# Eight of thirteen field pairs spread by DMA instead of seven, with a new order of the dump, the row loads, the gathers and the first tile

## The chip, the cores and the metric

The kernel runs on one core of one Trainium2 chip. The metric is the time of one execution on the device in microseconds (us), as the median of several runs. The engines of a core are TensorE (PE), VectorE (DVE), ScalarE (ACT), GpSimd (POOL) and SyncE (SP, which only issues DMAs here). Sixteen DMA engines move data between the chip's memory (HBM) and the core's SBUF. TensorE writes its results to PSUM.

## The reference, cut to what matters

It is an xDeepFM recommender with a batch of 2048, 26 sparse fields with embeddings of 32 numbers, and 13 dense numbers:

```python
emb = tables[feat_idx, sparse]                      # (2048, 26, 32)
linear_out = lin_sparse_w[feat_idx, sparse].sum(-1) + dense @ lin_dense_w
x0 = emb; xk = emb; res = []
for w, bb in ((conv1_w, conv1_b), (conv2_w, conv2_b)):
    h = xk.shape[1]                                 # 26, then 64
    hp = einsum('bhd,bmd->bhmd', xk, x0).reshape(-1, h * M, E)
    xn = sigmoid(einsum('oi,bid->bod', w, hp) + bb[None, :, None])
    half = xn.shape[1] // 2                         # 64
    xk = xn[:, :half]
    res.append(xn[:, half:])
cin_out = (concatenate(res, axis=1).sum(-1) @ cin_w + cin_b)[:, 0]
h1 = tanh(deep_x @ W1 + b1)                         # 845 -> 1024, deep_x is emb and dense
h2 = tanh(h1 @ W2 + b2); h3 = tanh(h2 @ W3 + b3)    # 512, 256
return linear_out + cin_out + (h3 @ deep_w + deep_b)[:, 0] + bias[0]
```

The second layer's products dominate: for each batch row and each of 32 embedding places, 64 values of `xk` times 26 of `x0`, contracted with a 128 x 1664 matrix. All is float32.

## The kernel before

**Tiles and steps.** The batch is cut into 16 tiles of 128 rows, and each tile into 4 steps of 8 embedding places (`STEP_D`); a step has 8 x 128 = 1024 columns. In a step, both halves of the 128 partitions hold the 64 values of `xk`, and one of 13 *pairs* of fields is laid beside them: the first field of the pair for one half of the partitions, the second for the other. So a pair takes one DVE multiplication of 128 x 1024 (L747) and a contraction on PE (`contract`, L800), which adds all 13 pairs into one accumulator. `ORDER` says which fields a pair number stands for.

**Laying out a pair.** The fields' values have to be repeated over 64 partitions. For the pairs in `BY_PE` PE does that with a matmul by 0/1 weights from the rows `x0t` into a PSUM slot `bc` (`spread_pair`, L780), from a 32-row quarter for each half of the columns (`group_of` says which quarters). DVE reads the slot and writes `hp`. For the pairs in `BY_DMA` the SP queue copies the field's row of 4 KB from HBM (`x0_rows`) into each of 64 partitions of `xb` (`spread_by_dma`, L501), in four groups (`COPIED`); DVE multiplies in place. The buffer of a pair is free when it has been contracted, and only then SP asks for the next step's copy (`sp.wait_ge(contracted, ...)`).

**The K part.** The first layer is symmetric, so it is computed from squares of sums of two fields: `spread_sum` (L787) fills three slots (`("K", 0..2)`), ACT squares them (L979), and PE contracts them in two column halves (`contract_k`, L794, "first"). ACT reads each half with a sigmoid (`read_xn`, L984 to L986): twice into `xk` for the next step and once into `r1`. PE's contractions of the step's own first five pairs ("of_this") wait for the read of half 0 (`xn_read`), since they start the accumulator that it frees. `read_y2` (L990) reads the finished accumulator of the step before into `r2`; the second K half waits for it. POOL adds up `r1` and `r2` (`add_up`).

**The order on PE** is written out in `STEP_WORK`: K fills, contractions 5 to 7 of the step before, turning the next tile's embeddings ("D"), contractions 8 to 12, pairs 0 to 2 spread, K contraction in two halves, pairs 5 to 7 spread, contractions 0 to 4. The slots `bc` are used in turn (`SLOTS` is 3).

**The next tile.** POOL gathers 26 fields of 128 rows into `emb` (L572), each gather tied to a multiplication (`gather_in`). In one step of a tile (`deep_step`: step 2 of the first tile, step 1 of the others; none in the last) PE transposes `emb` (`turn_deep`, L772) in three fills. ACT copies the result to `deep_t` and, rounded to float32r, to `deep_halves` (L975, L976), DVE computes the remainder (`lower_deep`, L698). SP then writes `deep_t` to `x0_rows` (`dump`, L438) and ACT writes both halves to `x0_halves` (`dump_halves`, L997, L999), ahead of its read of K half 1 in steps 1. From `x0_halves` ACT's queue loads `x0t` two steps ahead (`load_rows`, L388), four DMAs a step. In step 2 of a tile these are the first rows of the next tile, and they wait for the dump (`halves_dumped`); ACT issues them there behind `read_y2`.

**Queues.** Each engine works its instructions in order, the issue of DMAs too. SP: per step the four groups of spreads, then the row dump, and in the last two tiles the loads of `x_full` and `x_rest` (`load_x`, L490) for the deep layers, which run after all tiles.

## Time and profile before

| | |
|---|---|
| median of 3 runs | 1602.87 us (1598.68 to 1613.62) |
| the profiled execution's own time | 1607.53 us |
| its span | 1605.7 us |
| PE / DVE / ACT / POOL busy | 94% / 71% / 40% / 43% of the span |
| DMA moved | 322.08 MB, mean 201 GB/s |

The profile is one execution. "Busy" of an engine is the time in which it works an instruction; idle time is given with the instruction before which it stood, and with what ended it. The DMA share is the mean busy share of the 16 DMA engines. A step of a tile is measured from one K fill (L787) to the next; the first K fill of step 1 of tile 0 is at 80.30 us, and step 0 of tile 1 opens at 148.89.

### The profile page before, as it was taken

Reading aid. Unit: us, or ns where it says so; the run is one execution under the profiler, and the core shown is the slowest. Engines: PE = TensorE matmul, PEld = TensorE weight load, DVE = VectorE, ACT = ScalarE, POOL = GpSimd, SP = SyncE. Lnnn points to the kernel's source line nnn. Section 1 sums busy time; section 2 is a strip of 40 time slices with the busy share of each in tenths; the row PEclk is TensorE's granted clock in tenths of the full one; section 3 lists DMA queues with packets and bytes.
Section 4 is the critical chain, followed back from the end, with each engine's and each line's share of the span. In section 5 each row is a group of like instructions: output and inputs, shape, how many; then the busy total and the mean of one; then the engine's idle time right before and its main releaser. Section 6 shows DMA issues by size and latency. Waiting matters only on the chain.

```text
span 1605.7 us, 23632 instructions
## 1 busy us (share of the span) xinstructions
PE 1515.2 (94%) x6552; PEld 662.5 (41%) x6552; DVE 1133.7 (71%) x1113; ACT 646.7 (40%) x904; POOL 682.6 (43%) x600
## 2 busy tenths in 40 slices
PE   0598999999999999999999999999999999999999
PEld 0233333333333333333333333333333337787876
DVE  3385878788888887878787877788876785343442
ACT  2333443444444344334444443434443433444443
POOL 7356564546464646454555546464631010000000
PEclk9998999999999999999999999999999999999999
DMA  6686989888998899988898989898999993846741
GB/s 130 132 228 170 230 217 222 197 232 204 241 216 233 201 232 198 233 200 232 206 241 208 236 198 236 203 247 200 246 194 240 234 243 105 187 129 167 166 134 53
DMA packets 177869, 322.08 MB, mean 201 GB/s; under 512 B 30160, under 2 KB 106032, under 8 KB 177796
## 3 DMA queue, kind: packets, MB, share of 16 engines
q1 hardware_dynamic: 128250, 287.98, 70.8%
q10 hardware_dynamic: 36273, 26.61, 6.9%
q0 software_dynamic: 13312, 7.06, 4.4%
q8 instruction: 18, 0.29, 0.1%
q14 instruction: 16, 0.13, 0.0%
HBM read 300.24 MB, written 21.31 MB: 200 GB/s over the span
## 4 chain that ended last, share of the span: by engine, by line
PE 75%; DMA 9%; issue 4%; DVE 3%; SPq 2%; ACTq 2%; POOL 2%; ACT 1%; another core or an unknown queue 0%; DVEq 0%; POOLq 0%
PE acc L800 37%; PE acc L794 16%; PE bc L937 14%; DMA x0t<-x_halves 6%; PE bc L780 4%; PE bc L787 3%; ACTq L388 2%; POOL emb L572 2%; DMA emb<-table,idx_stage 2%; SPq L490 1%; DVE xb L747 1%; DVE hp L747 1%; DMA x_halves<-deep_halves 1%; PE bc L772 1%; DMA xb<-x_rows 1%
## 5 line engine op out<-in xcount | busy, mean ns | idle before, releaser
L572 POOL DMA_INDIRECT emb<-table,idx_stage x416 | 494.8, 1189 | 335.9 <-DVE hp L747 169.9
L747 DVE TENSOR_TENSOR hp<-bc,xk 128x1024 f32<-128x1024 f32 x384 | 446.3, 1217 | 257.1 <-PE bc L780 172.7
L747 DVE TENSOR_TENSOR xb<-xb,xk 128x1024 f32<-128x1024 f32 x448 | 552.4, 1288 | 15.1 <-DMA xb<-x_rows 14.9
L800 PE MATMUL acc<-xb,w2s 128*64 128x512 f32 x1792 | 408.6, 594 | 0.2
L800 PE MATMUL acc<-hp,w2s 128*64 128x512 f32 x1536 | 362.9, 608 | 6.0 <-ACT r L986 6.0
L794 PE MATMUL acc<-sq,w1s 128*128 128x512 f32 x768 | 349.9, 605 | 2.2 <-issue 2.2
L979 ACT ACTIVATE sq<-bc 128x1024 f32<-128x1024 f32 x192 | 182.9, 1027 | 190.2 <-PE bc L787 144.0
L800 PEld LDWEIGHTS acc<-xb,w2s 128*64 128x64 f32 x1792 | 127.1, 137 | 253.3 <-issue 227.0
L583 POOL TENSOR_TENSOR r<-r 128x512 f32<-128x512 f32 x96 | 128.8, 1342 | 220.6 <-ACT r L990 130.3
L794 PEld LDWEIGHTS acc<-sq,w1s 128*128 128x128 f32 x768 | 141.9, 191 | 181.3 <-issue 181.3
L984 ACT ACTIVATE xk<-acc,bias 64x512 f32<-64x512 f32 x128 | 87.3, 682 | 275.9 <-PE acc L794 164.1
L800 PEld LDWEIGHTS acc<-hp,w2s 128*64 128x64 f32 x1536 | 99.9, 138 | 202.8 <-issue 164.2
L990 ACT ACTIVATE r<-acc,bias 128x512 f32<-128x512 f32 x64 | 44.0, 687 | 285.5 <-PE acc L800 266.9
L937 PE MATMUL bc<-x_full,w_hi 128*128 128x512 f32 x384 | 125.2, 394 | 5.0 <-DVE w_lo L712 2.0
L762 DVE TENSOR_TENSOR h_lo<-h_raw,h_hi 128x512 fp32r<-128x512 f32 x48 | 33.2, 692 | 135.7 <-ACT h_hi L1109 135.7
L780 PE MATMUL bc<-x0t,sel 32*128 32x512 f32 x768 | 94.3, 462 | 5.4 <-ACT sq L979 4.2
L986 ACT ACTIVATE r<-acc,bias 64x512 f32<-64x512 f32 x128 | 87.4, 683 | 3.2
L1107 ACT ACTIVATE h_raw<-bc,bd 128x512 f32<-128x512 f32 x48 | 33.1, 689 | 137.1 <-PE bc L937 137.1
L985 ACT ACTIVATE xk<-acc,bias 64x512 f32<-64x512 f32 x128 | 87.1, 681 | 1.6
L787 PE MATMUL bc<-x0t,sel 64*128 64x512 f32 x384 | 63.0, 433 | 25.8 <-DMA x0t<-x_halves 14.2
L937 PEld LDWEIGHTS bc<-x_full,w_hi 128*128 128x128 f32 x384 | 72.2, 188 | 23.5 <-issue 7.1
L780 PEld LDWEIGHTS bc<-x0t,sel 32*128 32x128 f32 x768 | 38.1, 183 | 105.6 <-issue 57.9
(61 smaller groups left out, 814.0 us busy)
## 6 DMA issues: line engine op xcount, KB each, us to landing
xb<-x_rows SPq DMA_DIRECT2D x448, 256.0 KB
xb<-x_rows SPq DMA_DIRECT2D x192, 512.0 KB
w_raw<-W SPq DMA_DIRECT2D x48, 512.0 KB
xb<-x_rows SPq DMA_DIRECT2D x128, 128.0 KB
x0t<-x_halves ACTq DMA_DIRECT2D x252, 52.0 KB
x_full<-x_halves SPq DMA_DIRECT2D x96, 128.0 KB
x_halves<-deep_halves ACTq DMA_DIRECT2D x30, 384.0 KB
emb<-table,idx_stage POOLq DMA_INDIRECT x416
```

The lines of the kernel that those rows point to most:

```text
L572: nc.gpsimd.indirect_dma_start(out=emb[:, m, :], out_offset=None, in_=table, in_offset=bass.IndirectOffsetOnAxis(ap=idx_stage[:, m:m + 1], ...
L583: nc.gpsimd.tensor_tensor(total, r[:, 0, :] if sl == 1 else total, r[:, sl, :], ALU.add).then_inc(step, 1)
L747: nc.vector.tensor_tensor(product(n)[:, :], x[:, :], xk[sl % 2][:, :], ALU.mult).then_inc(multiplied, 1)
L780: last = nc.tensor.matmul(bc[slot][:, c * CHUNK:(c + 1) * CHUNK], sel[rows, ORDER[n], :], x[rows, :], start=True, stop=True)
L787: last = nc.tensor.matmul(bc[slot][:, c * CHUNK:(c + 1) * CHUNK], sel[rows, PAIRS + k, :], x[rows, :], start=True, stop=True)
L794: last = nc.tensor.matmul(acc_k[:, :], w1s[:, k, :], sq[k][:, cols], start=(k == 0), stop=(k == K1 - 1))
L800: last = nc.tensor.matmul(acc_y[H * c:H * c + H, :], w2s[:, ORDER[n], :], src[:, c * CHUNK:(c + 1) * CHUNK], start=(n == 0), stop=(n == PA ...
L937: last = nc.tensor.matmul(bc[a % 2][:, 0:CHUNK], w, x, start=(k == 0 and i == 0), stop=(k == rows - 1 and i == len(passes) - 1))
L979: nc.scalar.activation(sq[k][:, :], bc[slot][:, :], ACT.Square).then_inc(squared, 1)
L984: nc.scalar.activation(xk[slot][0:H, cols], xn[0:H, :], ACT.Sigmoid, bias=bias1[0:H, :])
L985: nc.scalar.activation(xk[slot][H:P, cols], xn[0:H, :], ACT.Sigmoid, bias=bias1[0:H, :]).then_inc(xk_made, 1)
L986: nc.scalar.activation(r1[H * c:H * c + H, sl, :], xn[H:P, :], ACT.Sigmoid, bias=bias1[H:P, :]).then_inc(xn_read, 1)
```

## The change

`BY_PE` becomes (0, 1, 2, 5, 6) and `BY_DMA` has eight pairs in four groups of two, (3, 4), (7, 8), (9, 10), (11, 12); `ORDER` is rearranged so that neighbouring PE pairs still lie in different quarters. The second spread of a step is one pair shorter. The turn of the embeddings is one fill of one slot instead of three (`TURNS`). It is in step 1 of every tile that has one, also of the first, which gets an order of its own there (`FIRST_TILE_WORK`), and DVE lowers the halves behind its multiplication 4 in that step. In the first tile the dump of the halves is issued by SP, behind the first spread of step 2; in the others by ACT, now directly behind `read_y2` and so ahead of both K reads. The row loads of step 2 stand ahead of `read_y2`. The gathers are timed anew and end a step earlier. One of the dense remainders moves from an `hp` buffer to `xb[7]`, and SP waits for its dump before the first tile.

```diff
@@ -63,10 +63,10 @@
 PER_GROUP = 16
-ORDER = [0, 8, 1, 3, 4, 9, 2, 10, 5, 6, 7, 11, 12]
-BY_PE = (0, 1, 2, 5, 6, 7)
+ORDER = [0, 8, 1, 3, 4, 9, 2, 5, 6, 7, 10, 11, 12]
+BY_PE = (0, 1, 2, 5, 6)
 assert sorted(ORDER) == list(range(PAIRS))
-COPIED = ((3, 4), (8, 9), (10, 11), (12,))
+COPIED = ((3, 4), (7, 8), (9, 10), (11, 12))
 BY_DMA = tuple(n for ns in COPIED for n in ns)
@@ -75,45 +75,59 @@
 STEP_WORK = (
     ("fill", (("K", 0), ("K", 1), ("K", 2))),
-    ("of_last", (5, 6, 7)),
-    ("fill", (("D", 0), ("D", 1), ("D", 2))),
-    ("of_last", (8, 9, 10, 11, 12)),
+    ("of_last", (5, 6, 7, 8)),
+    ("fill", (("D", 0),)),
+    ("of_last", (9, 10, 11, 12)),
     ("fill", (0, 1, 2)),
     ("first", 0),
     ("first", 1),
-    ("fill", (5, 6, 7)),
+    ("fill", (5, 6)),
     ("of_this", (0, 1, 2, 3, 4)),
 )
 FINAL_WORK = (
     ("fill", (0, 1, 2)),
     ("of_last", (5, 6, 7, 8, 9, 10, 11, 12)),
-    ("fill", (5, 6, 7)),
+    ("fill", (5, 6)),
     ("of_this", (0, 1)),
     ("terms", None),
     ("of_this", (2, 3, 4)),
 )
+
+FIRST_TILE_WORK = (
+    ("fill", (("K", 0), ("K", 1), ("K", 2))),
+    ("of_last", (5, 6, 7, 8)),
+    ("of_last", (9, 10, 11, 12)),
+    ("fill", (0, 1, 2)),
+    ("first", 0),
+    ("fill", (("D", 0),)),
+    ("first", 1),
+    ("of_this", (0, 1)),
+    ("fill", (5, 6)),
+    ("of_this", (2, 3, 4)),
+)
+DEEP_STEP = 1
 LEFT = tuple(n for kind, what in STEP_WORK if kind == "of_last" for n in what)
 DEEP_PARTS = range(0, 3), range(3, KD - 1), range(KD - 1, KD)
+
+TURNS = ((0, 1, 2),)
 SLOTS = 3
 PRO_FILLS = 6
 DUMPS = 2
 HALF_DUMPS = 3
-def deep_step(ahead):
-
-    return 2 if ahead == 3 else 1
+def step_work(sl, ahead):
+
+    if ahead == 0 and sl == STEPS - 1:
+        return FINAL_WORK
+    return FIRST_TILE_WORK if ahead == 3 and sl == DEEP_STEP else STEP_WORK
 def step_fills(sl, ahead):
-    fills = [use for kind, what in STEP_WORK if kind == "fill" for use in what]
-    if ahead == 0 and sl == STEPS - 1:
-        fills = [use for use in fills if not is_k(use)]
-    if ahead == 0 or sl != deep_step(ahead):
-        fills = [use for use in fills if not is_d(use)]
-    return fills
+    fills = [use for kind, what in step_work(sl, ahead) if kind == "fill" for use in what]
+    return fills if ahead > 0 and sl == DEEP_STEP else [use for use in fills if not is_d(use)]
 def is_k(use):
@@ -239,7 +253,7 @@
         diag_w = xb_all[0:M, 0:2 * M * P]
         diag = xb_all[0:M, 2 * M * P:(2 * M + 1) * P]
         dense_hi = [hp[2 + i][0:ND, :].bitcast(F32R) for i in range(2)]
-        dense_lo = [hp[4 + i][0:ND, :].bitcast(F32R) for i in range(2)]
+        dense_lo = [x[0:ND, :].bitcast(F32R) for x in (hp[4], xb[7])]
         x0t = [sc(f"x0t{i}", [P, CHUNK], F32R) for i in range(STEPS)]
@@ -388,6 +402,14 @@
                 eng.dma_start(x0t[sl][start:start + 2 * M:2, :].bitcast(F32),
                               rows[:, first:first + Q, :].rearrange("m d b -> m (d b)")).then_inc(x0_loaded[sl % 2], 16)
+
+        def dump_halves(eng, t):
+            for i in range(2):
+                eng.dma_start(x0_halves[bass.ds(t, 1), i, 0:(KD - 1) * P, :].rearrange("t (k p) b -> p (t k) b", p=P),
+                              deep_halves[:, i, 0:KD - 1, :].bitcast(F32)).then_inc(halves_dumped, 16)
+            eng.dma_start(x0_halves[bass.ds(t, 1), :, (KD - 1) * P:M * ROW, :].rearrange("t i p b -> p (t i) b"),
+                          deep_halves[0:LAST_E, :, KD - 1, :].bitcast(F32)).then_inc(halves_dumped, 16)
+
         W1_STEPS = 6
@@ -508,7 +530,11 @@
                             sp.wait_ge(contracted, contracted_by(s - 1, ns[-1]))
                             hold()
                         spread_by_dma(t, sl, i)
-                    if sl == deep_step(ahead) and ahead > 0:
+                        if is_first and sl == DEEP_STEP + 1 and i == 0:
+                            sp.wait_ge(deep_lowered, 2 * DEEP_N)
+                            hold()
+                            dump_halves(sp, t + 1)
+                    if sl == DEEP_STEP and ahead > 0:
                         dump(t + 1)
@@ -529,6 +555,7 @@
                 load_rows(sp, 0, sl, 0)
             sp.wait_ge(w1_step, W1_STEPS)
+            sp.wait_ge(dense_dumped, 64)
             sp.wait_ge(first_rows, FIRST_ROWS)
@@ -612,40 +639,42 @@
                 if is_first:
                     free_emb(t, DEEP_N)
                     gather(range(8), gathered)
-                    gather_in(s, range(8, 16), range(8))
+
+                    for m, (signal, count) in enumerate(((k_contracted, 1), (xk_made, 1), (xk_made, 2), (squared, K1 + 1),
+                                                         (squared, K1 + 2), (squared, 2 * K1))):
+                        pool.wait_ge(signal, count)
+                        hold()
+                        gather((8 + m,), gathered)
+                    gather_in(s, range(14, M), (0, 1, 2, 3, 4, 4, 4, 4, 5, 6, 7, 8))
                     add_up(t, 1, r1, r1_step, xn_read, 2, sum1)
-                    gather_in(s, range(16, 21), range(8, PAIRS))
-                    gather_in(s + 1, range(21, M), range(5))
                     add_up(t, 2, r1, r1_step, xn_read, 2, sum1)
+                    free_emb(t + 1, filled_by(t, DEEP_STEP, ("D", len(TURNS) - 1), ahead))
                     add_up(t, 1, r2, r2_step, y2_read, 1, sum2)
-                    free_emb(t + 1, filled_by(t, 2, ("D", DEEP_N - 1), ahead))
                     gather_in(s + 2, range(5), (1, 2, 3, 4, 6))
                     add_up(t, 3, r1, r1_step, xn_read, 2, sum1)
                     gather_in(s + 2, range(5, 11), range(7, PAIRS))
                     add_up(t, 2, r2, r2_step, y2_read, 1, sum2)
-                    gather_in(s + 3, range(11, 20), range(9))
+                    gather_in(s + 3, range(11, 22), (0, 1, 1, 2, 3, 3, 4, 5, 6, 7, 7))
                     return
                 if ahead > 0:
-                    gather_in(s - 1, range(20, 23), (8, 10, 12))
+                    gather_in(s - 1, range(22, M), (8, 9, 10, 12))
                 add_up(t - 1, STEPS - 1, r2, r2_step, y2_read, 1, sum2)
-                if ahead > 0:
-                    gather_in(s, range(23, M), (0, 1, 3))
                 add_up(t, 1, r1, r1_step, xn_read, 2, sum1)
                 if ahead > 1:
-                    free_emb(t + 1, filled_by(t, 1, ("D", DEEP_N - 1), ahead))
+                    free_emb(t + 1, filled_by(t, 1, ("D", len(TURNS) - 1), ahead))
                     gather_in(s + 1, range(4), (0, 2, 4, 6))
                 add_up(t, 2, r1, r1_step, xn_read, 2, sum1)
                 if ahead > 1:
                     gather_in(s + 1, range(4, 8), (7, 8, 10, 12))
                 add_up(t, 1, r2, r2_step, y2_read, 1, sum2)
                 if ahead > 1:
-                    gather_in(s + 2, range(8, 11), (0, 2, 4))
+                    gather_in(s + 2, range(8, 12), (0, 2, 4, 6))
                 add_up(t, 3, r1, r1_step, xn_read, 2, sum1)
                 if ahead > 1:
-                    gather_in(s + 2, range(11, 15), (7, 8, 10, 12))
+                    gather_in(s + 2, range(12, 17), (7, 8, 9, 10, 12))
                 add_up(t, 2, r2, r2_step, y2_read, 1, sum2)
                 if ahead > 1:
-                    gather_in(s + 3, range(15, 20), (0, 2, 4, 6, 7))
+                    gather_in(s + 3, range(17, 22), (0, 2, 4, 6, 7))
             over_tiles(pool, tile)
@@ -726,7 +755,7 @@
                     s = t * STEPS + sl
                     start = is_first and sl == 0
                     for n in range(PAIRS):
-                        if n == 0 and sl == deep_step(ahead) and ahead > 0:
+                        if n == (5 if is_first else 0) and sl == DEEP_STEP and ahead > 0:
                             dve.wait_ge(gathered, t * GATHERED + GATHERED)
...
@@ -828,7 +857,7 @@
                 else:
                     if use[1] == 0:
                         pe.wait_ge(gathered, t * GATHERED + GATHERED)
-                    turn_deep(slot, DEEP_PARTS[use[1]])
+                    turn_deep(slot, [k for part in TURNS[use[1]] for k in DEEP_PARTS[part]])
             pe.wait_ge(ident_loaded, IDENT_LOADED)
...
@@ -968,10 +997,11 @@
             upper_w(0, 0)
-            def turned_deep(slot, part):
+            def turned_deep(slot, part, first_k):
                 ks = DEEP_PARTS[part]
                 rows = rows_of(ks)
-                src = bc[slot][rows, 0:len(ks) * P].rearrange("p (k b) -> p k b", b=P)
+                at = (ks[0] - first_k) * P
+                src = bc[slot][rows, at:at + len(ks) * P].rearrange("p (k b) -> p k b", b=P)
                 nc.scalar.activation(deep_t[rows, ks[0]:ks[-1] + 1, :], src, ACT.Copy).then_inc(deep_copied, 1)
@@ -989,20 +1019,10 @@
                 act.wait_ge(contracted, s * PAIRS + PAIRS)
                 nc.scalar.activation(r2[:, sl, :], acc[sl % 2][:, :], ACT.Sigmoid, bias=bias2[:, :]).then_inc(y2_read, 1)
-
-            def dump_halves(t):
-                act.wait_ge(deep_lowered, t * DEEP_N + DEEP_N)
-                act.sem_inc(act_held, 1)
-                for i in range(2):
-                    act.dma_start(x0_halves[bass.ds(t, 1), i, 0:(KD - 1) * P, :].rearrange("t (k p) b -> p (t k) b", p=P),
-                                 deep_halves[:, i, 0:KD - 1, :].bitcast(F32)).then_inc(halves_dumped, 16)
-                act.dma_start(x0_halves[bass.ds(t, 1), :, (KD - 1) * P:M * ROW, :].rearrange("t i p b -> p (t i) b"),
-                             deep_halves[0:LAST_E, :, KD - 1, :].bitcast(F32)).then_inc(halves_dumped, 16)
-
             act.wait_ge(ident_loaded, IDENT_LOADED)
             for i in range(DEEP_N):
                 act.wait_ge(filled, i + 1)
-                turned_deep(i, i)
+                turned_deep(i, i, DEEP_PARTS[i][0])
             act.wait_ge(first_halves, FIRST_HALVES)
@@ -1020,10 +1040,6 @@
                     s = t * STEPS + sl
                     start = is_first and sl == 0
                     there = step_fills(sl, ahead)
-                    turning = sl == deep_step(ahead) and ahead > 0
-
-                    late = turning and sl == 2
-
                     def load_next_rows():
@@ -1033,8 +1049,8 @@
                             for c in range(2):
                                 load_rows(act, t + (sl + 2) // STEPS, (sl + 2) % STEPS, c)
-                    for kind, what in STEP_WORK:
-                        if kind == "of_last" and what[-1] == PAIRS - 1 and ("K", 0) in there and sl != 2:
+                    for kind, what in step_work(sl, ahead):
+                        if kind == "of_last" and what[-1] == PAIRS - 1 and ("K", 0) in there:
                             load_next_rows()
@@ -1051,23 +1067,19 @@
                                         else:
                                             act.wait_ge(dumped, t * (16 * DUMPS))
                                             act.wait_ge(halves_dumped, t * (16 * HALF_DUMPS))
-                                    turned_deep(slot_of(sl, use, ahead), use[1])
+                                    for part in TURNS[use[1]]:
+                                        turned_deep(slot_of(sl, use, ahead), part, DEEP_PARTS[TURNS[use[1]][0]][0])
                         elif kind == "of_last" and what[-1] == PAIRS - 1 and not start:
                             if sl == 1 and not is_first:
                                 act.wait_ge(r2_step, t * SUMS - (SUMS - 1))
                             if sl == STEPS - 1 and not is_first:
                                 act.wait_ge(r2_step, t * SUMS - (SUMS - (STEPS - 1)))
-                            if late:
-                                dump_halves(t + 1)
                             read_y2(s - 1, (sl - 1) % STEPS)
-
-                            if sl == 2 and not late:
-                                load_next_rows()
+                            if sl == DEEP_STEP and ahead > 0 and not is_first:
+                                act.wait_ge(deep_lowered, t * DEEP_N + 2 * DEEP_N)
+                                act.sem_inc(act_held, 1)
+                                dump_halves(act, t + 1)
                         elif kind == "first" and ("K", 0) in there:
-                            if turning and not late and what == 1:
-                                dump_halves(t + 1)
-                            if late and what == 1:
-                                load_next_rows()
                             act.wait_ge(k_contracted, k_contracted_by(s, what))
```

## Rows read from the trace of the kernel before

**Rows 1.** The page: busy shares, and groups with busy, mean ns, idle before.

```profile
PE 1515.2 (94%) x6552; PEld 662.5 (41%) x6552; DVE 1133.7 (71%) x1113; ACT 646.7 (40%) x904; POOL 682.6 (43%) x600
...
L747 DVE TENSOR_TENSOR xb<-xb,xk 128x1024 f32<-128x1024 f32 x448 | 552.4, 1288 | 15.1 <-DMA xb<-x_rows 14.9
...
L780 PE MATMUL bc<-x0t,sel 32*128 32x512 f32 x768 | 94.3, 462 | 5.4 <-ACT sq L979 4.2
```

**Rows 2.** The timeline of PE in one step: start us, us, what, idle before.

```profile
602.33 0.98 PE L787 MATMUL bc<-x0t,sel 64*128 64x512 f32 x6 [1.39 <-DMA x0t<-x_halves]
...
610.25 0.73 PE L780 MATMUL bc<-x0t,sel 32*128 32x512 f32 x6
610.91 5.42 PE L794 MATMUL acc<-sq,w1s 128*128 128x512 f32 x12
```

**Rows 3.** Windows by step: length, busy PE PEld DVE ACT POOL, PEclk, DMA share, GB/s.

```profile
99.33:126.95 27.62, 20.16 (x91) 7.49 (x90) 21.70 (x22) 9.33 (x16) 6.22 (x7) 0.93 0.84 235
126.95:148.89 21.94, 21.93 (x82) 7.74 (x82) 9.78 (x9) 7.89 (x11) 15.57 (x16) 0.86 0.57 137
...
542.00:561.03 19.03, 19.03 (x86) 6.84 (x84) 14.97 (x14) 7.63 (x10) 13.42 (x11) 1.00 0.93 201
561.03:581.25 20.22, 20.16 (x93) 7.47 (x91) 16.39 (x18) 9.09 (x16) 4.34 (x5) 1.00 0.85 195
581.25:602.33 21.08, 19.16 (x85) 6.83 (x83) 18.05 (x15) 8.15 (x11) 15.09 (x12) 1.00 1.02 260
602.33:621.36 19.03, 19.03 (x82) 6.83 (x82) 14.18 (x13) 7.63 (x10) 11.57 (x11) 1.00 0.88 212
```

**Rows 4.** Windows of twelve tiles and of the last two; queues: packets, MB, share.

```profile
208.29:1151.35 943.06, 929.12 (x4022) 335.61 (x4022) 757.57 (x672) 390.01 (x552) 519.14 (x444) 1.00 0.90 220
1151.35:1310.00 158.65, 155.85 (x669) 55.53 (x667) 121.66 (x109) 63.04 (x86) 39.49 (x36) 0.99 0.99 225
...
q1 hardware_dynamic: 62891, 181.47, 75.2%
q10 hardware_dynamic: 28644, 20.78, 9.1%
```

**Rows 5.** Waits of PE in the same twelve tiles: us in total, times, longest.

```profile
PE bc L787 <- DMA x0t<-x_halves: 6.8, 8, 1.7
PE acc L800 <- ACT r L986: 4.1, 3, 2.8
```

**Rows 6.** Windows of two steps beside the x loads, columns as in 3.

```profile
1210.23:1233.84 23.61, 21.50 (x86) 6.99 (x84) 15.08 (x15) 8.95 (x12) 5.00 (x5) 0.93 1.05 255
...
1271.89:1290.92 19.03, 19.03 (x85) 6.83 (x83) 14.91 (x15) 7.64 (x10) 1.27 (x1) 1.00 1.08 246
```

**Rows 7.** Timeline of ACT, its queue and PE in a step 1; line L999 (min/median/max ns).

```profile
570.25 0.69 ACT L990 ACTIVATE r<-acc,bias 128x512 f32<-128x512 f32 x1 [2.78 <-PE acc L800]
...
575.52 4.03 ACTq L999 DMA_DIRECT2D x_halves<-deep_halves  x1
...
576.80 2.80 PE L800 MATMUL acc<-hp,w2s 128*64 128x512 f32 x12
...
579.67 0.68 ACT L984 ACTIVATE xk<-acc,bias 64x512 f32<-64x512 f32 x1 [3.76 <-issue]
...
L999 ACTq DMA_DIRECT2D x_halves<-deep_halves x15: 1053/3597/6312, 107.4 to 1203.8; - x15
```

**Rows 8.** The chain that ended last, around 593 us: start, us, what.

```profile
593.31 8.97 DMA x0t<-x_halves
```

**Rows 9.** The first tile: a piece of the chain; the timeline of POOL and ACT.

```profile
107.38 14.39 DMA x_halves<-deep_halves
...
69.94 0.95 POOL L572 DMA_INDIRECT emb<-table,idx_stage  x1 [15.47 <-DVE hp L747]
71.19 0.95 POOL L572 DMA_INDIRECT emb<-table,idx_stage  x1 [0.30 <-issue]
...
125.13 0.68 ACT L984 ACTIVATE xk<-acc,bias 64x512 f32<-64x512 f32 x1 [11.20 <-issue]
```

4 lines of the change are left out of this document (2 added, 2 removed).

## The prediction

> **What bounds the kernel now.** I read the busy shares first: TensorE (PE) 94%, VectorE (DVE) 71%, ScalarE (ACT) 40% [rows 1]. The timeline of PE inside one step of the product part shows it going from the fill of the K part through contractions, a spread of three pairs (0.73 us), the K part's 12 matmuls and on, without idle time but the one before the fill [rows 2]. The table by step gives 19.03 us for steps 0 and 3 of a tile and 20.22 for step 1, which also turns the next tile's embeddings (1.2 us of it, seven transposes); with 19.03 for step 2 a tile would be 77.3 us [rows 3]. Twelve whole tiles took 943.06 us, 78.6 each, at a DMA share of 0.90 [rows 4]. So PE sets 77.3 of 78.6 us. The DMA engines are the second resource: 0.90 x 78.6 = 70.7 us of work of all 16 per tile. By step [rows 3] (share times length, scaled by 70.7/73.2 to the mean tile) it is 17.1, 16.6, 20.8 and 16.2 us; step 2, with the dump of the next tile, is at 1.02. The waits of PE in those tiles are mostly 6.8 us for loads of x0t and 4.1 us for ACT's reads [rows 5].
>
> **One pair less on PE.** Three pairs are spread in 0.66 us (610.25 to 610.91) by 6 matmuls [rows 2]. At 462 ns each [rows 1] one after another they would take 2.8 us, so those of different row quarters run together; neighbouring pairs lie in opposite halves, hence three pairs are two rounds of 0.33 us and two pairs one. I take 0.33 us a step (bounds 0.22, a third of 0.66, and 0.33). The pair's contraction stays. A tile's floor on PE becomes 77.3 - 1.3 = 76.0 us. DVE multiplies the pair from SBUF instead of PSUM, one instruction either way; it is busy 15.0 of 19.03 us [rows 3], and that idle time covers a small difference: nothing.
>
> **One pair more by DMA.** The SP queue, q1, takes 75.2% of 943.06 us, 14.8 us in each of 48 steps, and moves 181 MB [rows 4]. Twelve row dumps of 429 KB are 5 MB of them, so seven pairs are 14.4 us and one is 2.05 us of all engines. A tile's work becomes 70.7 + 8.2 = 78.9 us, against a floor of 76.0. What decides is how much work the engines do per microsecond of time. Shares of 1.05 and 1.08 were held for 19 to 24 us, beside x loads in small pieces, and 1.02 in a step 2 [rows 3, 6]. I take 1.03, nearest to that last row, which has the same mix (bounds 1.00 and 1.08).
> In bytes: those three stretches moved 246 to 260 GB/s, and eight pairs make 220 GB/s x 19.65 us + 0.52 MB = 4.85 MB a step, 18.7 to 19.7 us. The Trainium skill, page "DMA: Bandwidth & Descriptors", section "Specifications", gives about 358 GB/s as the HBM limit of one core; by it the same bytes would need an estimated 13.5 us and the change would go as in the first rival. No row here comes near that rate over a step, and the sum goes by the rows.
>
> **ACT's dump moved ahead of its first read.** Now ACT reads y2 (570.25) and xk's half 0, and then issues the three DMAs of the halves' dump. The third holds ACT's queue for 4.03 us, so that half 1 is read only at 579.67, 3.76 us late [rows 7]. Nobody waits for half 1 then. Over 15 tiles that issue takes 1.05 to 6.3 us, 3.6 in the median [rows 7]. In the new order all three stand between the read of y2 and that of half 0, and PE's contractions 0 to 4 wait for exactly this read (`xn_read`). From 570.9 (570.25 and its 0.69): 1.3 us for the first two issues, as they end before the third at 575.52, and 3.6 make 575.8; three activations of 0.7 end at 577.9. PE would be ready at 576.80 - 0.33 = 576.5 [rows 7]. That is 1.4, and I take 1.5 us a tile in step 1. Bounds: 0, if the issue holds the queue as little as its minimum of 1.05, and 4.5, if it ends no sooner than now. Behind it in ACT's queue stands the read of half 1, which nobody awaits, and the squares of the K fill at 581.25, which it doesn't reach but at the upper bound.
> What the move buys: the dump's data flow earlier. The ACT queue, q10, works 9.1% of the stretch, 7.2 us a tile, and half its bytes are the dump [rows 4]; up to 3.6 us of DMA work leaves step 2 for step 1, and I take half, 1.8. In step 2 the loads of the next tile's first x0t no longer stand behind the read of y2, about 9 us into the step, but behind three squares, about 5 us sooner. Now the last of them is issued at 593.31 and lands at 602.28 for a fill due at 600.9 [rows 2, 8]. That stall, 6.8 us in twelve tiles, goes; late next are the spreads of xb.
>
> **Middle tile, summed.** Step 0: DMA 19.2/1.03 = 18.6, so PE's 18.7, and 18.8 with some unevenness. Step 1: DMA (18.6 + 1.8)/1.03 = 19.8; PE 20.2 - 0.33 + 1.5 = 21.4. Step 2: (22.8 - 1.8)/1.03 = 20.4, of which 0.4 is caught up in step 3: 20.0. Step 3: DMA 17.7, so PE's 18.7. Together 78.9 against 78.6, +0.3: over 13 tiles **+4 us** (with the bounds of its terms it is the rivals' tile).
>
> **First tile.** Its turn moves from step 2 to step 1. Step 2 is 27.62 us now: the dump's last DMA takes 14.39 us to land, ACT stands 11.20 us for it. Step 3 is 21.94 us, with the granted clock at 0.86 after that idle time [rows 3, 9]. In the new order step 1 gains the turn (19.03 + 1.2 - 0.33 = 19.9). The dump goes out on SP after the first spread of step 2, at about 101.5 to 104, and lands 5 to 14 us later; ACT waits for it ahead of y2, so x0t is asked for at 110 to 118, and of that the 11 us until PE wants y2 cover the first part. I take 22.0 for step 2 and 18.7 for step 3: 27.62 + 21.94 + 19.03 = 68.6 become 60.6, **-8 us** (bounds -3, the dump as slow as now, and -11, no wait left). The gathers must now be done at about 91, not 103. POOL idles 15.47 us before the ninth; six are moved into that gap, and at 0.95 + 0.30 us each the other twelve end near 85 [rows 9]: nothing, unless they land over 5 us later, which would cost PE what is over. Behind the dump in SP's queue are pairs 7 and 8; they slip about 4 us and are due 13 us after they are free: nothing. SP's new wait for the dense dumps is for transfers of the start, long landed when it is reached: nothing.
>
> **Gathers and groups.** The last gathers of later tiles end a step sooner. The pairs (7, 8) are asked for after contraction 8 and needed after seven multiplications, no tighter than (8, 9) now. Nothing for both.
>
> **Last two tiles.** Here SP also loads x: 0.99 x 158.65 = 157.1 us of work [rows 4]. Eight steps with one pair more add 16.4; at 1.05, the share of these steps [rows 6], 165.2 us, **+6.5** (bounds -8, PE alone and the excess of the 23.61 us step gone, and +15, share 1.00).
>
> Sum: +4 - 8 + 6.5 = +2.5 on the profiled execution's 1607.5, 1610. The median of the runs shown is 4.7 us under that execution, hence **1605**. The deep layers that follow aren't touched.
>
> **Rivals**, all against the median.
> 1. Faster: the engines carry the eighth pair as they carry seven, and ACT's wait is nil. Middle tile 76.2 (-2.4 x 13), first -11, last two -8: -50, **1553**. For it: the ordinary steps' shares of 0.85 to 0.93, and the 1.08. Against: 1.02 in step 2 already. It is also the page's rule. 0.22.
> 2. Faster: as forecast, but ACT's queue isn't held. Step 1 is 19.9, a tile 77.4: -16 - 8 + 5, **1584**. Against it stands the median of 3.6 us. 0.12.
> 3. Slower: the engines give a share of 1.00. Its place is DVE's wait for xb. A tile is 19.2 + 21.4 + 21.0 + 18.7 = 80.3, +22; first -7; last two +15: +30, **1633**. It decides from a share under about 1.02. For it: 0.90 is all that the middle tiles show on average, and spreads can only be asked for when their buffer is free. 0.22.
> 4. Slower: ACT's third issue ends where it ends now, 3 us more in 14 tiles, +42: **1647**. 0.10.
> The forecast's own case has 0.34 and spans 1590 to 1619.
>
> What a measurement of this kernel can tell from no change is about 1%, 1587 and 1619. Faster: rivals 1 and 2 but for an edge, 0.32. Slower: rivals 3 and 4, 0.32. Same: 0.36. The range cuts rivals 1 and 4 by half each: 1554 to 1646.
>
> **What would show it.** Right: DVE's idle time for DMA xb, 14.9 us now [rows 1], grows beyond 50; the DMA share of the middle tiles is 1.00 or more; PE waits 1 to 2 us for ACT's r once a tile, in step 1; spreads of two pairs take 0.33 us; waits for x0t are gone behind the first tile; the K fill that opens tile 1 comes near 141 us, not at 148.89. Wrong: tiles of 76 us at a share below 1 are rival 1; a step 1 of 24 us is rival 4; a first tile that waits for gathers breaks its term.

## The result, and the profile after

The changed kernel takes 1699.26 us (median of 4 runs, 1682.09 to 1706.57), the kernel before 1604.05 us beside it: a ratio of 1.057, 95% interval 1.048 to 1.067. It is about 90 us slower, not the same. The profiled execution took 1699.54 us; its span is 1697.7 us against 1605.7. (In the experiments below some executions were disturbed ones, which no ratio uses, among them the profiled ones of two kernels, the one with the dump behind both K reads and the first with the row loads a step earlier; of these only the pattern of steps and issues is used.)

The page of the changed kernel; columns as in [rows 1] (L776 is DVE's multiplication, L829 the contraction, L809 the spread of pairs on PE):

```profile
PE 1539.3 (91%) x6424; PEld 661.7 (39%) x6424; DVE 1159.8 (68%) x1113; ACT 646.5 (38%) x904; POOL 678.2 (40%) x600
...
L776 DVE TENSOR_TENSOR xb<-xb,xk 128x1024 f32<-128x1024 f32 x512 | 651.1, 1327 | 48.7 <-DMA xb<-x_rows 43.0
...
L829 PE MATMUL acc<-hp,w2s 128*64 128x512 f32 x1280 | 331.0, 650 | 69.4 <-ACT r L1016 65.7
...
L809 PE MATMUL bc<-x0t,sel 32*128 32x512 f32 x640 | 80.6, 482 | 5.5 <-ACT sq L1009 4.2
```

DVE waits longer for the copies (43.0 us, from 14.9), as an eighth pair by DMA would let one expect. But the new item is the third line: PE stands 65.7 us in front of contractions of `hp`, the pairs 0 to 2, and what releases it is ACT's read of the K part's half 0. It was 4.1 us in twelve tiles [rows 5] and 6.0 us in the whole execution before.

The windows of the changed kernel, columns as in [rows 3]: steps 0 to 3 of a middle tile, the long step 1 near the end, the thirteen tiles 1 to 13, and step 2 of the first tile.

```profile
568.30:587.10 18.80, 18.80 (x82) 6.72 (x80) 15.38 (x14) 7.64 (x10) 11.13 (x10) 1.00 1.02 246
587.10:613.40 26.30, 21.66 (x89) 7.74 (x87) 22.88 (x22) 9.60 (x16) 7.90 (x8) 0.94 0.86 228
613.40:632.20 18.80, 18.80 (x82) 6.72 (x80) 10.00 (x9) 7.63 (x10) 7.90 (x8) 1.00 0.95 232
632.20:651.00 18.80, 18.80 (x82) 6.69 (x80) 17.05 (x14) 7.64 (x10) 15.52 (x14) 1.00 0.98 250
...
1266.16:1299.18 33.02, 25.81 (x89) 8.69 (x87) 22.46 (x22) 9.59 (x16) 1.27 (x1) 0.79 0.95 219
...
147.39:1244.77 1097.38, 1025.01 (x4255) 363.91 (x4253) 844.42 (x729) 422.63 (x598) 563.61 (x489) 0.97 0.94 229
...
104.48:128.60 24.12, 20.76 (x84) 7.22 (x82) 16.64 (x15) 7.53 (x10) 6.29 (x7) 0.93 0.96 252
```

The ordinary steps got shorter, from 19.03 to 18.80 us [rows 3], and the step with the dump is 26.30 instead of 20.22. A tile is 1097.38 / 13 = 84.4 us, from 78.6. The mean steps 0 to 3 of those thirteen tiles, K fill to K fill, are 19.9, 26.4, 18.8 and 19.3 us; before they were 19.1, 20.2, 20.1 and 19.1. On the span: 13 x 5.83 = 75.8 us in these tiles, -1.5 in the first (its K fill of tile 1 came at 147.39, not 148.89), 12.5 in the last two (12.2 of it in the one step 1 of 33.02 us, which was 20.8), 5.1 behind the last K fill. The sum is 91.9 of the 92.0.

The timeline of ACT, its queue, SP's queue and PE in the step 1 from 587.10, as in [rows 7] (L523 issues the spreads, L1020 reads y2, L408 and L410 issue the dump, L1014 to L1016 read a K half, L823 contracts the K part):

```profile
587.45 11.10 SPq L523 DMA_DIRECT2D xb<-x_rows  x12
...
596.78 5.42 PE L823 MATMUL acc<-sq,w1s 128*128 128x512 f32 x12
...
596.82 0.69 ACT L1020 ACTIVATE r<-acc,bias 128x512 f32<-128x512 f32 x1 [2.07 <-PE acc L829]
597.14 1.17 ACTq L408 DMA_DIRECT2D x_halves<-deep_halves  x2
598.46 6.30 ACTq L410 DMA_DIRECT2D x_halves<-deep_halves  x1
602.12 0.51 PE L809 MATMUL bc<-x0t,sel 32*128 32x512 f32 x4
605.14 0.68 ACT L1014 ACTIVATE xk<-acc,bias 64x512 f32<-64x512 f32 x1 [7.63 <-DVE hp L776]
606.54 0.68 ACT L1016 ACTIVATE r<-acc,bias 64x512 f32<-64x512 f32 x1
607.27 4.49 PE L829 MATMUL acc<-hp,w2s 128*64 128x512 f32 x12 [4.64 <-ACT r L1016]
611.60 1.89 PE L829 MATMUL acc<-xb,w2s 128*64 128x512 f32 x8
```

The third issue begins 1.64 us behind the read of y2 and ends at 604.76, 7.9 us behind it. Before, it began 5.3 us behind that read and ended 9.3 us behind it [rows 7]. Moved 3.6 us forward, it ends only 1.4 us sooner: it got longer. SP's queue in the step of [rows 7] before shows what it met:

```profile
561.33 12.54 SPq L501 DMA_DIRECT2D xb<-x_rows  x12
```

There SP's twelfth spread had been issued 1.65 us before the third issue began; now the two fall together (598.55 and 598.46). Over the fourteen steps of this kind in each kernel, counted from the end of SP's twelfth issue, the third issue of the dump began 1.7 us behind before and begins 0.1 us ahead now, and it ended 5.3 us behind before and ends 5.7 us behind now (medians). The beginning moved, the end hardly did.

PE is idle for 4.64 us, and then its 12 contractions take 4.49 us where the same 12 took 2.80. The granted clock was 0.94 in this step, so part of it ran at the lower level (1.2 of 2.4 GHz) behind the idle time. 4.64 and 1.69 are 6.3 of the 6.4 us by which this step is over the 19.9 that it takes without the wait, in the first experiment below. The name behind the idle time of L1014 (DVE hp) is the last semaphore that it wanted; what it stood for was ACT's queue. The third issue over all tiles (min/median/max ns):

```profile
L410 ACTq DMA_DIRECT2D x_halves<-deep_halves x14: 4823/5772/10144, 182.0 to 1280.1; - x14
```

The one of 10.1 us is in the step of 33.02 us.

### The profile page after: what moved, and what is told of

The parts are those of the page before. It is cut to its first block and busy times, and to the rows that moved or that the text cites. A ratio compares the mean times of both kernels' runs of the same rounds, so it can differ in the third digit from the quotient of the medians.

```text
span 1697.7 us, 23223 instructions
## 1 busy us (share of the span) xinstructions
PE 1539.3 (91%) x6424; PEld 661.7 (39%) x6424; DVE 1159.8 (68%) x1113; ACT 646.5 (38%) x904; POOL 678.2 (40%) x600
## 2 busy tenths in 40 slices
DMA packets 186061, 355.63 MB, mean 209 GB/s; under 512 B 30160, under 2 KB 106032, under 8 KB 185988
## 5 line engine op out<-in xcount | busy, mean ns | idle before, releaser
L776 DVE TENSOR_TENSOR xb<-xb,xk 128x1024 f32<-128x1024 f32 x512 | 651.1, 1327 | 48.7 <-DMA xb<-x_rows 43.0
L599 POOL DMA_INDIRECT emb<-table,idx_stage x416 | 475.3, 1142 | 323.4 <-DVE hp L776 149.4
L776 DVE TENSOR_TENSOR hp<-bc,xk 128x1024 f32<-128x1024 f32 x320 | 373.9, 1218 | 285.1 <-PE bc L809 219.9
L829 PE MATMUL acc<-xb,w2s 128*64 128x512 f32 x2048 | 473.8, 598 | 18.4 <-DVE xb L776 15.1
L829 PE MATMUL acc<-hp,w2s 128*64 128x512 f32 x1280 | 331.0, 650 | 69.4 <-ACT r L1016 65.7
L823 PE MATMUL acc<-sq,w1s 128*128 128x512 f32 x768 | 358.0, 616 | 5.5 <-ACT r L1020 3.4
L829 PEld LDWEIGHTS acc<-xb,w2s 128*64 128x64 f32 x2048 | 144.2, 138 | 319.5 <-issue 249.8
L823 PEld LDWEIGHTS acc<-sq,w1s 128*128 128x128 f32 x768 | 144.5, 195 | 189.9 <-issue 185.7
L1014 ACT ACTIVATE xk<-acc,bias 64x512 f32<-64x512 f32 x128 | 87.3, 682 | 283.9 <-PE acc L823 130.5
L829 PEld LDWEIGHTS acc<-hp,w2s 128*64 128x64 f32 x1280 | 86.1, 146 | 236.7 <-issue 142.9
L1020 ACT ACTIVATE r<-acc,bias 128x512 f32<-128x512 f32 x64 | 44.0, 687 | 306.6 <-PE acc L829 208.6
L1016 ACT ACTIVATE r<-acc,bias 64x512 f32<-64x512 f32 x128 | 87.5, 683 | 3.2
L809 PE MATMUL bc<-x0t,sel 32*128 32x512 f32 x640 | 80.6, 482 | 5.5 <-ACT sq L1009 4.2
L966 PE MATMUL bc<-x_full,w_lo 128*128 128x512 f32 x192 | 75.1, 391 | 0.0
L809 PEld LDWEIGHTS bc<-x0t,sel 32*128 32x128 f32 x640 | 31.8, 185 | 108.0 <-issue 68.6
```

The source lines that it names most:

```text
L599: nc.gpsimd.indirect_dma_start(out=emb[:, m, :], out_offset=None, in_=table, in_offset=bass.IndirectOffsetOnAxis(ap=idx_stage[:, m:m + 1], ...
L776: nc.vector.tensor_tensor(product(n)[:, :], x[:, :], xk[sl % 2][:, :], ALU.mult).then_inc(multiplied, 1)
L809: last = nc.tensor.matmul(bc[slot][:, c * CHUNK:(c + 1) * CHUNK], sel[rows, ORDER[n], :], x[rows, :], start=True, stop=True)
L823: last = nc.tensor.matmul(acc_k[:, :], w1s[:, k, :], sq[k][:, cols], start=(k == 0), stop=(k == K1 - 1))
L829: last = nc.tensor.matmul(acc_y[H * c:H * c + H, :], w2s[:, ORDER[n], :], src[:, c * CHUNK:(c + 1) * CHUNK], start=(n == 0), stop=(n == PA ...
L966: last = nc.tensor.matmul(bc[a % 2][:, 0:CHUNK], w, x, start=(k == 0 and i == 0), stop=(k == rows - 1 and i == len(passes) - 1))
```

## Experiments

Three questions: is it the place of the dump (with the issue that holds ACT) or the eighth copy that costs the time; what is left of each when the other is mended; and what holds the third issue. Each ratio is against the kernel before, on the same chip.

### The dump's place, with eight copies

**Between the two K reads**, where it was:

```diff
                             read_y2(s - 1, (sl - 1) % STEPS)
-                            if sl == DEEP_STEP and ahead > 0 and not is_first:
+                        elif kind == "first" and ("K", 0) in there:
+                            if what == 1 and sl == DEEP_STEP and ahead > 0 and not is_first:
                                 act.wait_ge(deep_lowered, t * DEEP_N + 2 * DEEP_N)
                                 act.sem_inc(act_held, 1)
                                 dump_halves(act, t + 1)
-                        elif kind == "first" and ("K", 0) in there:
```

> The changed kernel with one thing put back: in tiles 1 to 14 ACT issues the dump of the halves between its two K reads, as before the change, and not ahead of both. Theory Q (ACT's queue is held by the dump's third issue, 5 to 8 us in the changed kernel's trace, and PE waits for the read of half 0 behind it): step 1 of a tile falls from 26.3 us to about 20, 14 x 6.3 = 88 us go, 1600 to 1620 us. Theory D (the eighth pair fills the DMA engines and that is the loss): step 1 stays long, the DMA work only waits elsewhere, 1680 us or more.

1647.3 us, ratio 1.021 (1.014 to 1.027), 27 us over what was expected at most. 3.6 of the 5.7% are gone. Source, waits and timeline of that kernel:

```profile
L410 ACTq DMA_DIRECT2D x_halves<-deep_halves x14: 2902/3730/6930, 183.2 to 1236.6; - x14
...
PE acc L823 <- ACT r L1020: 29.8, 10, 7.4
PE acc L829 <- ACT r L1016: 7.3, 4, 3.5
...
514.54 3.56 ACTq L402 DMA_DIRECT2D x0t<-x_halves  x4
518.22 0.69 ACT L1020 ACTIVATE r<-acc,bias 128x512 f32<-128x512 f32 x1 [9.48 <-issue]
```

The third issue takes 3.7 us in the median, as in the kernel before (3.6) with seven copies. Steps 1 are 19.9 us, as expected. A new wait stands in steps 2: there the row loads are ahead of the read of y2 and want the dump to have landed, so ACT stands in front of y2 and PE's second K half behind it. The kernel before, with the loads behind y2, has no such wait.

**On SP**, behind the first spread of step 2, in every tile (ACT's dump is taken out):

```diff
-                        if is_first and sl == DEEP_STEP + 1 and i == 0:
-                            sp.wait_ge(deep_lowered, 2 * DEEP_N)
+                        if ahead > 0 and sl == DEEP_STEP + 1 and i == 0:
+                            sp.wait_ge(deep_lowered, t * DEEP_N + 2 * DEEP_N)
```

> The changed kernel, but all tiles dump the halves as its first tile does: SP issues them behind the first spread of step 2, and ACT issues none. Theory Q: no read of ACT stands behind an issue of a dump; step 1 is about 20 us. But the dump lands later and ACT waits for it in step 2 ahead of its read of y2, up to 4 us a tile as in the first tile: 1600 to 1650 us. Theory D: 1680 us or more, as the same bytes are moved.

1690.8 us, ratio 1.047 (1.040 to 1.055). By its time alone this would be theory D's case; the steps say otherwise. Steps 1 are mostly 19.9 again (20.6 in the mean, two of them 21.7 and 25.7), steps 2 are 21.7 to 28.4. PE waits 53.5 us behind ACT's read of y2: the same new wait, larger since the dump is later.

**Behind both K reads** on ACT (the same lines are taken out behind the read of y2):

```diff
                             read_xn((sl + 1) % 2, (sl + 1) % STEPS, what)
+                            if what == 1 and sl == DEEP_STEP and ahead > 0 and not is_first:
+                                act.wait_ge(deep_lowered, t * DEEP_N + 2 * DEEP_N)
+                                act.sem_inc(act_held, 1)
+                                dump_halves(act, t + 1)
```

> The changed kernel, but ACT issues the dump of the halves behind both K reads of step 1. Theory Q: both reads come in time; behind the dump in ACT's queue stand now the squares of the next K fill, which have about 6 us of slack until PE contracts them; step 1 is about 20 us and step 2 18.8 to 21: 1595 to 1630 us. Theory D: 1680 us or more.

1668.06 us (1629.86 to 1683.15), where 1595 to 1630 was expected. The runs scatter too widely for a ratio with an interval, so this only fits the two others: its long steps are steps 2 too, up to 34 us.

**The kernel before with the dump ahead of both reads**, seven copies:

```diff
                             read_y2(s - 1, (sl - 1) % STEPS)
+                            if turning and not late:
+                                dump_halves(t + 1)
...
-                            if turning and not late and what == 1:
-                                dump_halves(t + 1)
```

> The kernel before with one thing changed: seven pairs by DMA and six by PE stay, but in tiles 1 to 14 ACT issues the dump of the halves right behind the read of y2, ahead of both K reads. Theory Q: PE waits for the read of half 0 in every step 1, by the 3.0 to 6.3 us that the third issue takes in the kernel before less the 3 us of slack, and some clock loss behind it: 14 times 2 to 6 us, 1630 to 1690 us. Theory D: no pair was added, 1604 us within 10.

1648.73 us, ratio 1.023 (1.016 to 1.029). Its source, waits, window of its longest step 1 and PE in it:

```profile
L999 ACTq DMA_DIRECT2D x_halves<-deep_halves x15: 1057/4877/6937, 109.3 to 1239.7; - x15
...
PE acc L800 <- ACT r L986: 32.0, 13, 3.7
...
658.77:686.68 27.91, 23.17 (x92) 8.13 (x90) 22.18 (x22) 9.59 (x16) 8.91 (x8) 0.88 0.78 202
...
679.29 5.39 PE L800 MATMUL acc<-hp,w2s 128*64 128x512 f32 x12 [3.35 <-ACT r L986]
```

This one edit, in a kernel whose DMA engines are busy 0.84 through the thirteen tiles, costs 2.3%, by the same lengthened issue (4.9 us instead of 3.6) and the same wait. Its steps 1 are 24.3 us in the mean, from 20.2; its steps 2 fall from 20.1 to 19.1, which gives a part back. So the place of the dump costs time by itself, in either kernel; with the eighth copy it costs more.

### Both orders mended, then the eighth copy taken away

The dump between the reads, and the loads of step 2 behind y2 again:

```diff
-                        if kind == "of_last" and what[-1] == PAIRS - 1 and ("K", 0) in there:
+                        if kind == "of_last" and what[-1] == PAIRS - 1 and ("K", 0) in there and sl != 2:
                             load_next_rows()
...
                             read_y2(s - 1, (sl - 1) % STEPS)
+                            if sl == 2:
+                                load_next_rows()
```

> The changed kernel with both moves in ACT's queue put back: the dump between the two K reads (as in a_mid) and the row loads of step 2 behind the read of y2. In a_mid PE waited 29.8 us before the second K half for y2, ACT standing at the dump's semaphore ahead of it. Theory Q2 (what a_mid still lost is again ACT's queue, this time its wait for the dump): 30 to 40 us less than a_mid, about 1605 to 1618 us. Theory D (the engines are full and the lateness is theirs): within 10 us of a_mid's 1647.

1635.61 us, ratio 1.018 (1.012 to 1.024), between the two expectations. The wait for L1020 is gone; whether the time fell against the kernel with the dump alone mended, these intervals do not tell. ACT's queue is not free of waits either. PE still stands 15.9 us in front of L829 for ACT's read of half 0, longest in a step 2 of 27.1 us: there ACT has read y2 at 978.3 and issues the row loads, which want the dump to have landed, only at 985.2, its K read comes at 989.0, and PE stands 6.4 us for it. The same kernel with the copy of pair 12 left out behind the first step (the pair is still multiplied and contracted, from what its buffer holds, so that the output is another):

```diff
                 ns = COPIED[i]
+                if i == 3 and not first_step:
+                    ns = ns[:1]
```

> As a_mid_y2, but the copy of pair 12 is left out after the first step (DVE multiplies what stands there, so its part of the sum is not the reference's); PE spreads five pairs and DMA seven. What the eighth copy costs beside the rest: Theory D: DVE's waits for xb, some 50 us in a_mid, fall to under 15, and the time is 20 to 40 us under a_mid_y2, near 1580 us (63 x 0.23 us under the kernel before and the first tile's gain). Theory Q2: 0 to 12 us under a_mid_y2.

1575.32 us, ratio 0.981 (0.974 to 0.988). The thirteen middle tiles of the two, and DVE's wait, first with eight copies:

```profile
144.38:1173.45 1029.07, 1003.42 (x4255) 357.52 (x4253) 834.34 (x731) 422.44 (x598) 561.64 (x489) 0.99 0.99 245
...
DVE xb L776 <- DMA xb<-x_rows: 64.5, 43, 3.1
```

and with seven:

```profile
145.98:1146.56 1000.58, 994.36 (x4255) 357.87 (x4253) 846.28 (x729) 422.69 (x598) 576.87 (x488) 1.00 0.90 225
...
DVE xb L778 <- DMA xb<-x_rows: 3.8, 5, 1.5
```

Same work on PE; 79.2 us a tile against 77.0. With the order mended the engines are at 0.99 through thirteen tiles, and they set the end. Of 48.3 us between the two spans 28.5 are in these tiles, 10.8 in the last two and 10.6 behind the last K fill, less 1.6 in the first. (With eight copies the profiled execution is the fastest of its four, 11 us under the median, so the medians lie 60 us apart and the spans 48.) PE's own waits shrink with the copy: for ACT's read of half 0 from 15.9 to 2.9 us, for a pair of `xb` from 15.5 to 0.3, for x0t from 6.0 to 3.5. So the copy's price comes through all of these and not through DVE alone. The eighth copy costs 3.7% (1.018 against 0.981), while one pair less on PE with the other orders would be worth 1.9% if its copy were free. It isn't.

**The orders alone**, with seven copies and six PE pairs (three fills for the turn), dump and loads as in the kernel with both mended (the fills and contractions in `STEP_WORK` follow the pairs):

```diff
-ORDER = [0, 8, 1, 3, 4, 9, 2, 5, 6, 7, 10, 11, 12]
-BY_PE = (0, 1, 2, 5, 6)
+ORDER = [0, 8, 1, 3, 4, 9, 2, 10, 5, 6, 7, 11, 12]
+BY_PE = (0, 1, 2, 5, 6, 7)
...
-COPIED = ((3, 4), (7, 8), (9, 10), (11, 12))
+COPIED = ((3, 4), (8, 9), (10, 11), (12,))
...
-TURNS = ((0, 1, 2),)
+TURNS = ((0,), (1,), (2,))
...
```

> The orders alone: seven pairs by DMA and six by PE as before, dump and row loads of ACT as before, but the first tile turned in step 1 with its dump on SP, and the gathers timed as in the change. It prices the rest of the change without the eighth pair: the first tile's 5 to 8 us and the gathers' 1 to 2 are gained, 1597 to 1612 us on the chip of the last call, 0.4 to 0.6% under the kernel before.

1608.39 us (10 runs), ratio 0.998 (0.995 to 1.002): no change. Its K fill of tile 1 came at 140.1 us, 8.8 sooner, and its middle tiles take 79.5 us instead of 78.6, which gives that back (the long ones are steps 2, 19 to 27 us).

### What holds the third issue

Two theories. Own queue (B in the expectations): the row loads of step 1 (four DMAs) stand ahead of the dump on ACT. Traffic (G): the bytes of the spreads are in the engines at that moment. First the row loads of step 1 a step earlier, behind the K reads of step 0:

```diff
-                        if sl < 2 or ahead > 0:
+                        if sl != 1 and (sl < 2 or ahead > 0):
...
                             read_xn((sl + 1) % 2, (sl + 1) % STEPS, what)
+                            if sl == 0 and what == 1:
+                                for c in range(2):
+                                    load_rows(act, t, 3, c)
```

> The changed kernel, but ACT issues the row loads that step 1 had (first used at the start of step 2) a step earlier, behind the two K reads of step 0. The dump stays ahead of the K reads of step 1. Theory B (the dump's third issue is long because row loads issued 4 to 8 us before still stand in ACT's queue): the issue is about 1 us, steps 1 are 19.9 us, and no spread is delayed as in a_x0sp: 1610 to 1635 us; what is left over the kernel before is the eighth copy's. Theory G (traffic of the spreads holds it): 5 us and more, 1680 us or more.

1669.27 us, ratio 1.036 (1.030 to 1.042). The same edit in the kernel of the orders alone with the dump early:

> Seven pairs by DMA and six by PE, the first tile and the gathers of the change, the dump ahead of the K reads as in the change, and the row loads of step 1 issued a step earlier by ACT. Theory B: the dump lands early, the loads of the next tile's first rows don't wait for it, and a tile is near PE's 77.2 us: 13 x 1.3 us and the first tile's 8 us under the kernel before, 1575 to 1592 us. Theory G: like b_early, 1635 us or more.

1619.92 us, ratio 1.009 (1.006 to 1.012). And in the kernel before with the dump early:

> The kernel before with two things: the dump ahead of both K reads of step 1 (as in b_early, which took 2.3% more), and the row loads of step 1 issued a step earlier, behind the K reads of step 0. Theory B: the hold of 4.9 us in b_early falls to about 1 and nothing of the 2.3% is left; the early dump lets the next loads come in time: 1580 to 1598 us. Theory G: as b_early, 1635 to 1650 us.

1624.44 us, ratio 1.011 (1.007 to 1.014), against 1.023 without the edit. The third issue has medians of 6.0, 4.2 and 4.2 us in the three. It does not fall to 1 us though no row load stands closely ahead of it any more: the own queue fails as the main cause. It is not nothing, though: in the kernel before, half of the 2.3% went with the row loads, and all three times lie between what the two theories expected. Then the loads on SP, behind the second spread of step 1 (ACT does not issue them):

```diff
                         spread_by_dma(t, sl, i)
+                        if sl == 1 and i == 1:
+                            for c in range(2):
+                                load_rows(sp, t, 3, c)
```

> The changed kernel, but the row loads of step 1 are issued by SP behind its second spread, not by ACT. The dump stays ahead of both K reads. Of what holds ACT's queue at the dump's third issue: Theory B (its own queue still holds row loads that haven't been moved when the dump's 768 + 768 pieces are added): the issue takes 1 to 2 us as on SP's queue in a_sp (1.1 us), the steps 1 come to 20 or 21 us, the time to 1620 to 1650 us. Theory G (whatever engine issues, it is the traffic of the spreads at that moment): it stays at 5 to 6 us and the time within 15 us of the changed kernel's.

1638.71 us, ratio 1.017 (1.010 to 1.023). Source, timeline of SP's and ACT's queues in one step 1, and waits:

```profile
L410 ACTq DMA_DIRECT2D x_halves<-deep_halves x14: 516/752/3677, 172.8 to 1220.4; - x14
...
560.82 6.18 SPq L523 DMA_DIRECT2D xb<-x_rows  x6
567.20 3.85 SPq L402 DMA_DIRECT2D x0t<-x_halves  x4
571.37 5.70 SPq L523 DMA_DIRECT2D xb<-x_rows  x6
...
DVE xb L779 <- DMA xb<-x_rows: 102.3, 73, 3.4
```

The third issue takes 0.75 us and steps 1 are 20.0, with the dump still ahead of both reads. But this edit changes two things: no row load stands in ACT's queue, and SP issues half of its spreads only behind the loads (in the changed kernel all twelve are issued from 587.45 to 598.55, by when the third issue of the dump begins). The late spreads then cost steps 3, which are 22.0 us in the mean: DVE waits 102.3 us. The engines' share is 1.00 through its thirteen tiles, at 240 GB/s. To part the two, one run takes bytes from the spreads, one from the row loads. In the first, the copies of pairs 7 to 12 in step 1 carry 16 of their 1024 columns; DMAs and pieces are as many as in the changed kernel (186061 packets in both), their data are mostly left out (306 MB instead of 356), so that the output is another:

```diff
+                cols = 16 if sl == 1 and i > 0 else COLS
...
-                    rows = rows.rearrange("t m d b -> t m (d b)").to_broadcast([parts.stop - parts.start, len(ns), COLS])
+                    rows = rows.rearrange("t m d b -> t m (d b)")[:, :, 0:cols].to_broadcast([parts.stop - parts.start, len(ns), cols])
```

> The changed kernel, but in step 1 of every tile the copies of the pairs 7 to 12 carry 16 of 1024 columns (their part of the result is not the reference's); the number of DMAs and of pieces is the same, the bytes are 1/64. Theory G (the dump's third issue is held by the traffic in the engines at that moment): it falls from 5.8 us to about 1, steps 1 to 20 us, and the time to 1600 to 1625 us. Theory B (ACT's own queue with the row loads): the issue stays at 4 to 6 us and the time above 1660 us.

1583.89 us, ratio 0.985 (0.980 to 0.990); the orders are those of the changed kernel. That is under the 1600 to 1625 expected. Eleven of its thirteen middle steps 1 are 19.9 us. The two others have no long issue: in the one of 27.8 us PE stands 4.9 us in front of the turn for a gather of POOL, in the one of 25.0 us 3.1 us for a pair of `xb`. Its source and a step 1:

```profile
L410 ACTq DMA_DIRECT2D x_halves<-deep_halves x14: 800/812/965, 176.5 to 1178.3; - x14
...
638.85 1.16 ACTq L408 DMA_DIRECT2D x_halves<-deep_halves  x2
640.16 0.81 ACTq L410 DMA_DIRECT2D x_halves<-deep_halves  x1
```

In the second, ACT's row loads of steps 0 and 1 carry 16 of 512 columns from tile 1 on (this output is another too):

```diff
+                cols = 16 if thin else CHUNK
...
-                                load_rows(act, t + (sl + 2) // STEPS, (sl + 2) % STEPS, c)
+                                load_rows(act, t + (sl + 2) // STEPS, (sl + 2) % STEPS, c, thin=sl < 2 and not is_first)
```

> The changed kernel, but ACT's row loads of steps 0 and 1 carry 16 of 512 columns from tile 1 on (the result is not the reference's); their number and pieces are the same. Theory B: the dump's third issue falls to about 1 us and the time to 1600 to 1630 us. Theory G: it stays at 5 to 6 us, the time above 1670 us.

1655.71 us, ratio 1.030 (1.025 to 1.035):

```profile
L411 ACTq DMA_DIRECT2D x_halves<-deep_halves x14: 3330/4924/7743, 178.0 to 1240.2; - x14
...
PE acc L830 <- ACT r L1017: 49.8, 14, 6.4
```

4.9 us against 0.81, in the median. The bytes of the spreads hold the issue, in all fourteen tiles; those of the row loads add about 0.9 of 5.8 us. The traffic theory is shown. (The time is under the 1670 us expected, since fewer bytes are moved: the share is 0.93.) What the sequencer stands for inside the issue, the trace does not name.

### A version faster than both

The orders alone with seven copies, the dump early, and the row loads of step 1 on SP, so that the spreads behind them come late where seven copies leave room (against the kernel of the orders alone; ACT leaves its loads of step 1 out):

```diff
                                 load_next_rows()
-                        elif kind == "first" and ("K", 0) in there:
-                            if what == 1 and sl == DEEP_STEP and ahead > 0 and not is_first:
+                            if sl == DEEP_STEP and ahead > 0 and not is_first:
...
-                        if sl < 2 or ahead > 0:
+                        if sl != 1 and (sl < 2 or ahead > 0):
...
+                        if sl == 1 and i == 1:
+                            for c in range(2):
+                                load_rows(sp, t, 3, c)
```

> Seven pairs by DMA and six by PE, the first tile, gathers and early dump of the change, and SP issues the row loads of step 1 behind its second spread (what brought the hold from 5.8 to 0.75 us in a_x0sp). If the hold goes here too, steps 1 are 20.1 us and steps 2 near 19.0, as the dump lands early: 1575 to 1592 us, under both kernels. If SP's 3 us of issuing make the spreads late with seven pairs too, 1605 us or more.

1597.15 us (9 runs), ratio 0.993 (0.990 to 0.996). Source, the thirteen middle tiles, and waits:

```profile
L410 ACTq DMA_DIRECT2D x_halves<-deep_halves x14: 986/1060/1424, 170.4 to 1195.0; - x14
...
140.84:1165.59 1024.75, 1009.87 (x4356) 364.22 (x4356) 835.64 (x729) 422.80 (x598) 573.09 (x487) 1.00 0.89 220
...
PE bc L819 <- DMA x0t<-x_halves: 14.5, 12, 2.0
DVE xb L779 <- DMA xb<-x_rows: 14.1, 17, 2.0
```

It beats the kernel before by 0.7%, a small gain with its interval below 1 and short of the 1575 to 1592 expected, and not by its middle tiles, which are 78.8 us against 78.6. Of the 9.0 us between the spans (1596.7 and 1605.7) 8.0 are the first tile, the term that the prediction gave the new order (K fill of tile 1 at 140.84, not 148.89), and 5.3 the last two; the middle tiles take back 3.3 and the end 1.1.

## Why the prediction was wrong

The forecast was 1605 us, no change; it is outside the range too (1646). Against its own sum the spans miss 89.5 us: 72 in the middle tiles, 6.5 in the first, 11 at the end.

**ACT's dump moved ahead of its first read: the step that failed.** The prediction placed the wait rightly (PE's contractions 0 to 4, released by ACT's r, in step 1) and priced it at 1.5 us a tile: it took the third issue's duration from where it stood, 3.6 us, and moved it as a block. That duration is no property of the instruction. It depends on how many of the spreads' bytes are in the engines, and the new place is where SP issues the last of its twelve; the old one was 1.7 us behind. So the issue began earlier but ended nearly as long behind SP's twelfth as before: 5.7 us, from 5.3 (medians of 14 steps; 6.4 with the dump between the reads, 3.1 with seven copies and the dump early, 0.7 with the spreads' bytes taken away). Measured: an issue of 5.8 us in the median, and in the step shown a wait of 4.6 us and 1.7 us more for contractions at the lower clock, which the sum did not have at all. A step 1 is 26.4 us, not 21.4: 65 us over 13 tiles. The rival with an issue that "ends where it ends now" had the mechanism and the wait (its bound of 4.5 us; the end behind the read of y2 went from 8.9 to 7.7 us in the median), but stopped at 1647 since it left out the clock and the eighth copy's price, and I gave it 0.10. With the dump mended alone the time falls by 3.6%, 58 us.

The Trainium skill, page "DMA: Bandwidth & Descriptors", section "Issuing engines are not separate DMA queues", calls the sequencer's time to initiate a DMA usually small beside the DMA. Here one such issue has a median of 5.8 us on ACT, and 0.8 us with the spreads' bytes taken away. In the kernel with the thin row loads, whose profile has the landing, such a DMA lands 12.0 us behind its issue and the issue itself takes 4.9. That isn't small beside it; the measurement decides.

**The eighth copy.** Its work was sized well: 0.99 x 79.2 = 78.4 us a tile in the mended kernel, forecast 78.9. (It is no fixed amount: with the row loads on SP the same bytes take 1.00 x 80.7 = 80.7 us a tile.) The share was not: 1.03 was taken, from a single step 2, where 0.99 is what thirteen tiles held with the ACT order mended. That is the third rival's case (1.00), and 1.00 is what the kernel with the row loads on SP held. In the changed kernel itself it is hidden partly behind the other wait: the share is 0.94, since the engines too get through work while PE stands. Steps 0 and 3 are 1.1 and 0.6 us over the forecast; step 2 is 18.8 instead of 20.0, for the dump is then long out. The end is +17.6 us against +6.5, of which 12.2 are the one step with the issue of 10.1 us; in the pair of kernels above, 21.4 us of the eighth copy's 48.3 are at the end.

**One pair less on PE.** 0.23 us a step, not 0.33: the four matmuls of two pairs take 0.51 us where six took 0.73 [rows 2]. Two pairs are not one round and three two. That was the lower bound; 13 tiles lose 5 us by it.

**The first tile.** Forecast -8, got -1.5 in the profiled execution. Of the 6.5 us missed, 2.5 lie ahead of step 1, whose K fill came at 82.79 and not 80.30 (79.1 to 82.3 in the other kernels, so this seems to be scatter), 1.8 in step 1 (21.7 us, forecast 19.9) and 2.1 in step 2 (24.1, forecast 22.0). In the twelve experiments with the new first tile the K fill of tile 1 came at 139.1 to 146.0 us, in six of them before 141.5. So the term is there, at 3 to 10 us; with one profiled execution of each, whether it varies by kernel or by execution stays open. Part of it is a wait that the prediction put at nothing: the gathers were to end near 85, but in the changed kernel the last issue ends at 89.7, as step 1 began 2.5 us late and three of the issues took 1.97 us and not 0.95. PE stands in front of the turn 3.2 us with both orders mended and 3.6 us with the copy left out, for a gather by the trace, and behind these waits half of the K contractions take 4.44 us instead of 2.74. In the changed kernel it stands 1.8 us there; the trace puts that down to DVE, so that the gather is not shown for this one. In the kernel with the thin spreads there is no wait at this place, and its step 1 is 19.7 us.

**x0t.** The stall of 6.8 us is gone, as forecast; it comes back in part once the loads are behind y2 again (6.0 us in the whole execution, where the kernel before has 14.2).

**Signs that were named.** DVE's wait beyond 50: 43.0 us. Share of 1.00: 0.94. Both were missed because PE's own wait took their place; with the orders mended they read 64.5 and 0.99, the second still just short of its sign.

Pieced together, by ratios: the order in ACT's queue 4.0% (1.057 against 1.018), 63 us; the eighth copy 3.7%, 59 us; what is left, a pair less on PE with the first tile, gains 1.9%, 31 us. 63 + 59 - 31 = 91 us. Each of the terms has about 1 point of uncertainty. The split holds along this path only: with seven copies the early dump alone costs 2.3%, so something under 2 points belong to the order and the eighth copy together.

## What to carry to other kernels

An issue of a DMA is an instruction with a queue behind it, and its duration is set by the traffic at the moment of issue: when it is moved in the program, read what other queues put into the engines just ahead of the new place, and take the longest durations of the row, not the median. Put nothing that the critical engine waits for behind such an issue, unless a trace with the new order shows it short there. Where a wait of several us appears in front of TensorE, add what the matmuls behind it lose at the lower clock. And a DMA share of 1.02 to 1.08 in a single step is no capacity for a whole stretch; 0.99 and 1.00 are what thirteen tiles held here.

## What the hardware showed beyond that

- The same 90 KB DMA issue took 0.5 to 10.1 us on ACT; on SP, at another moment, behind the first spread of step 2, it took 0.8 to 1.8 us with all eight pairs spread.
- Behind idle times of 3.35 and 4.64 us of PE the next twelve contractions took 5.39 and 4.49 us instead of 2.80, with the granted clock at 0.88 and 0.94 over the step: 2.6 and 1.7 us on top of the idle time.
- Through thirteen tiles the engines moved 245 GB/s at a share of 0.99 in one kernel and 240 at 1.00 in another, mostly rows of 4 KB. The Trainium skill, page "DMA: Bandwidth & Descriptors", section "Specifications", gives a limit of about 358 GB/s for a core's HBM traffic. No run here comes near it; with this mix the engines' own time is used up first.
